# Maxima of one unit and a lead as own + relu(other - own), and V of twelve heads and a weight merge among the score tiles

## The reference

```python
q = _split(lora_linear(x, Wq, bq, Bq, Aq))
k = _split(lora_linear(x, Wk, bk, Bk, Ak))
v = _split(lora_linear(x, Wv, bv, Bv, Av))
scores = jnp.einsum('bhqd,bhkd->bhqk', q, k) * SCALE
attn = jax.nn.softmax(scores, axis=-1)
out = jnp.einsum('bhqk,bhkd->bhqd', attn, v)
...
return lora_linear(out, Wo, bo, Bo, Ao)
```

## Time and profile before

| what | value |
|---|---|
| median of three runs | 350.2 us (345.63 to 353.56) |
| the profiled execution | 349.53 us |
| its span, first to last instruction | 347.7 us |
| TensorE busy | 322.9 us of the span, 1919 matmuls |
| VectorE busy | 280.4 us, of which 150.3 us are the 128 maximum reductions |
| ScalarE busy | 241.9 us, of which 134.2 us are the 256 exponentials |
| GpSimd busy | 128.5 us |

### The profile page before, as it was taken

How to read it: one execution, slowest core, us unless ns; L and a number is a source line. 1 busy time by engine, 2 the same in 40 slices (tenths; PEclk the granted TensorE clock), 3 DMA queues, 4 the chain that set the end, 5 groups by cost and what they waited for, 6 DMA issues and landing times.

```text
span 347.7 us, 5546 instructions
## 1 busy us (share of the span) xinstructions
PE 322.9 (93%) x1919; PEld 141.8 (41%) x1919; DVE 280.4 (81%) x471; ACT 241.9 (70%) x465; POOL 128.5 (37%) x133
## 2 busy tenths in 40 slices
PE   7999789999999999999999899999998789699796
PEld 3753343222222222222222244359545645447695
DVE  6466998999999999999999345338689987988774
ACT  1576112888888898989888867994779323668694
POOL 5032018999300000000023001301699949994030
PEclk9999998999999999999999999999999969879899
DMA  7936855354132000000000000000000000000011
GB/s 216 326 51 129 144 166 86 63 117 84 21 78 45 3 0 3 0 3 0 0 3 1 3 1 2 0 2 0 1 2 0 1 0 2 0 2 0 1 62 60
DMA packets 14879, 14.57 MB, mean 42 GB/s; under 512 B 5060, under 2 KB 13191, under 8 KB 14663
## 3 DMA queue, kind: packets, MB, share of 16 engines
q1 hardware_dynamic: 12422, 12.09, 15.4%
q10 hardware_dynamic: 2176, 1.64, 1.6%
q0 software_dynamic: 256, 0.52, 0.9%
HBM read 5.78 MB, written 1.05 MB: 20 GB/s over the span
## 4 chain that ended last, share of the span: by engine, by line
PE 69%; DVE 14%; ACT 8%; POOL 5%; issue 3%; ACTq 0%; DVEq 0%; POOLq 0%
PE ps L1450 17%; PE ps L1436 13%; DVE mx L1126 9%; PE ps L1412 7%; PE ps L1582 6%; PE ps L1594 6%; PE ps L1363 4%; POOL pbuf L777 3%; PE ps L1567 3%; PE ps L1393 2%; PE ps L1626 2%; ACT ps L958 1%; PE ps L1352 1%; PE ps L1331 1%; ACT parts L898 1%
## 5 line engine op out<-in xcount | busy, mean ns | idle before, releaser
L1126 DVE TENSOR_REDUCE mx<-ps 128x1 f32<-128x1024 f32 x128 | 150.3, 1219 | 5.1 <-PE ps L1412 4.0
L913 ACT ACTIVATE pbuf<-ps 128x512 f32<-128x512 f32 x256 | 134.2, 604 | 24.6 <-PE ps L1436 23.6
L1436 PE MATMUL ps<-pack 64*128 64x512 f16 x256 | 75.9, 382 | 3.0 <-ACT pbuf L913 1.9
L1450 PE MATMUL ps<-pbuf,v_slot 128*32 128x512 f32 x512 | 68.0, 604 | 1.3 <-ACT parts L898 1.3
L1412 PE MATMUL ps<-pack 64*128 64x512 f16 x256 | 62.2, 388 | 4.5 <-DVE mx L1126 4.3
L1436 PEld LDWEIGHTS ps<-pack 64*128 64x128 f16 x256 | 18.8, 93 | 76.8 <-ACT pbuf L913 53.4
L777 POOL TENSOR_TENSOR pbuf<-wT 128x1024 f32<-128x1024 f32 (+3 forms) x32 | 48.2, 1533 | 4.7 <-ACT wT L987 4.7
L732 POOL COPY v_slot<-v_sb 128x512 f32<-128x512 f32 x8 | 4.8, 612 | 108.9 <-PE ps L1450 87.4
L708 POOL TENSOR_TENSOR rstd<-rstd,minus_half 128x2 f32<-128x2 f32 x16 | 11.4, 713 | 71.3 <-DVE rstd L1043 71.3
L1220 DVE SCALAR_TENSOR_TENSOR pack<-ps,g_unit,pack 128x512 f16<-128x512 f32 (+1 forms) x40 | 24.7, 640 | 14.5 <-ACT pack L970 14.5
L1582 PE MATMUL ps<-v_sb,w_nat 128*128 128x512 f16 (+1 forms) x160 | 32.7, 351 | 1.8 <-DVE v_sb L1212 1.8
(11 more groups left out here) (143 smaller groups left out, 370.4 us busy)
## 6 DMA issues: line engine op xcount, KB each, us to landing
w_nat<-in_L_ffn_w_dram SPq DMA_DIRECT2D x2, 1024.0 KB, 7.4
pack<-pbuf SPq DMA_DIRECT2D x24, 64.0 KB, 3.1
pack<-pack SPq DMA_DIRECT2D x3, 512.0 KB, 4.3
x_res<-in_L_attn_a_x_dram SPq DMA_DIRECT2D x4, 256.0 KB, 3.8
pack<-parts SPq DMA_DIRECT2D x16, 64.0 KB, 2.4
pack<-parts SPq DMA_DIRECT2D x32, 32.0 KB, 2.0
out_dram<-x_res SPq DMA_DIRECT2D x4, 256.0 KB, 2.1
w_nat<-in_L_attn_b_Wqkv_dram ACTq DMA_DIRECT2D x1, 768.0 KB, 6.3
```

Of the source, the lines that this page charges most:

```text
L913: act.activation(pbuf[:, c % 2, j, :], ps[:, b, :], ACT.Exp, scale=scale_reg).then_inc(drained[b], 1)
L1126: dve.tensor_reduce(mx[:, par, k:k + 1], ps[:, b:b + 2, :].rearrange("p b k -> p (b k)"), AX_X, ALU.max) \
L1436: pe.matmul(ps[:, b, :], k_group[rows, at, j, P * c:P * c + P].rearrange("p g t -> p (g t)"), q_rows[rows, at, qh, j, :].rearrange("p g t ...
L1450: ins = pe.matmul(ps[32 * j:32 * j + 32, PV_BANK, :], v_slot[:, qh, c, j, :], pbuf[:, c % 2, j, :], start=(c == 0), stop=(c == TT - 1))
```

## The change

For 23 maximum tiles (`is_signed`: all 16 of unit 0 and the seven of the lead), GpSimd first negates the queries in the half of the rows that only maxima read (`turn`). One matmul over all 128 rows then gives own minus other, a second over the 64 own rows gives own. ScalarE writes relu(other - own) to SBUF (`take_over_own`, two slots in `over_own`, which share the place of `tern1`), and VectorE adds that to the own scores and keeps the running maximum (`tensor_tensor_reduce`). The other 105 tiles stay.

V is cut in two: heads 0 to 3 (64 columns) beside unit 0's maxima and the lead, heads 4 to 15 (192 columns) as entries of the ring in front of certain score tiles of units 0 and 1 (`BESIDE_SCORES`), and so is Wo's merge. The ring's banks are now numbered by key over all units (`ring_keys`). The merge of Wv moves behind the projections 4 and 5. The shift of unit 0 lands by ScalarE's own DMA queue; on SP's queue the later shifts move ahead of some heads of groups 2 and 3. The load of Wqkv moves from ScalarE's queue to SP's. The clock-holding matmuls of the lead are five in one place, not two behind each of five tiles. ScalarE's loop over units is written out. `first_halves` lies in `parts` and not in `pbuf`, so that ScalarE's first exponentials no longer wait for the DMAs that read it. The waits for a group's rows stand where its first maximum tile is issued.

```diff
-    yield ("wt", V_)
     yield ("proj", 4)
     yield ("proj", 5)
+    yield ("wt", V_)
-    return [("proj", 6), ("proj", 7), *(("v", t) for t in range(TT)), ("wsum",), ("shift",), ("wt", O_)]
+    return [key for behind in (*BESIDE_FIRST_UNIT, *BESIDE_LEAD) for key in behind]
...
+BESIDE_FIRST_UNIT = [[] for _ in range(FILLS)]
+BESIDE_FIRST_UNIT[1] = [("proj", 6)]
+BESIDE_FIRST_UNIT[3] = [("proj", 7)]
+for _t, _k in enumerate(range(5, FILLS, 2)):
+    BESIDE_FIRST_UNIT[_k] = [("v", 0, _t)]
+BESIDE_LEAD = [[], [("shift", 0), ("wsum",)], [("v", 0, TT - 2)], [("v", 0, TT - 1)]]
+
+
+BESIDE_SCORES = {
+    **{(0, 4 * n + 4): ("v", 1, n) for n in range(TT - 2)},
+    (1, 4): ("v", 1, TT - 2), (1, 8): ("v", 1, TT - 1), (1, 12): ("wt", O_),
+}
...
+def ring_keys(u):
+
+    for s in range(STEPS):
+        if (u, s) in BESIDE_SCORES:
+            yield BESIDE_SCORES[u, s]
+        if s == SHIFT_AT and u < NU - 1:
+            yield ("shift", u + 1)
+        yield ("score", u, s)
...
+def is_signed(u, k):
+
+    return isinstance(u, int) and (u == 0 or u == 1 and k < LEAD)
...
+        def land_shift(eng, g, qh, u):
+
+            is_drained(eng, ("shift", u))
+            n = G * TT // 2
+            for r in (0, 1):
+                rows = SHIFT_ROWS[g // 2]
+                rows = slice(ROWS * r + rows.start, ROWS * r + rows.stop, rows.step)
+                eng.dma_start(q_rows[rows, g, qh, 2 * r:2 * r + 2, :].rearrange("o h t -> o (h t)"),
+                              m_rows[n * r:n * r + n, :]).then_inc(shift_landed, 16)
...
-            pack_heads(2, 0, 1)
-            land_shift(0, 0, 0)
-            pack_heads(2, 1, G - 1)
+            pack_heads(2, 0, 3)
+            land_shift(sp, 0, 1, 1)
+            pack_heads(2, 3, 1)
             repeat_group(2)
-            land_shift(0, 1, 1)
+            pack_heads(3, 0, 2)
+            land_shift(sp, 1, 0, 2)
+            pack_heads(3, 2, 2)
+            repeat_group(3)
...
+            is_drained(sp, ("wt", V_))
+            sp.dma_start(wqkv[:, :, :], a["L0_attn_b_Wqkv"].rearrange("(c p) h n -> p c (h n)", p=P)) \
+                .then_inc(wqkv_in, 16)
...
+            def turn(rows, g, qh, first, last):
+
+                at = q_rows[rows, g, qh, :, :].rearrange("p j t -> p (j t)")[:, first:last]
+                pool.tensor_scalar(at, at, -1.0, 0.0, ALU.mult, ALU.add).then_inc(turned, 1)
+                turns[0] += 1
+                pool.wait_ge(turned, turns[0])
+
+            for j in range(G):
+                pool.wait_ge(head_packed_by_pool[j], 32)
+                other = 1 - score_rows(j)
+                turn(slice(ROWS * other, ROWS * other + ROWS), 0, 0, HALF * j, HALF * j + HALF)
...
+            pool.wait_ge(second_half_repeated, 16)
+            turn(slice(ROWS, 2 * ROWS), 0, 1, 0, P * LEAD)
...
+            def take_over_own(u, k):
+
+                b = PAIR_BANKS[k % 2]
+                act.wait_ge(filled[b], base[b] + u * (FILLS // 2) + (k // 2 + 1))
+                act.activation(over_own[:, k % 2, :], ps[:, b + 1, :], ACT.Relu, scale=-1.0).then_inc(over_own_ready, 1)
...
+            for k in range(FILLS):
+                take_over_own(0, k)
+                if k == 3:
+                    evacuate_weight(V_)
+                for key in BESIDE_FIRST_UNIT[k]:
+                    beside(key)
+            act.wait_ge(scale_ready, 1)
+            scale_reg = act.alloc_register("exp_scale_bits")
+            act.reg_load(scale_reg, exp_scale[0:1, 0:1].bitcast(U32))
+            for k in range(LEAD):
+                take_over_own(1, k)
+                for key in BESIDE_LEAD[k] if k < len(BESIDE_LEAD) else ():
+                    beside(key)
+                if k == 1:
+                    land_shift(act, 0, 0, 0)
+                if k >= LEAD - 4 and k < LEAD - 1:
+                    exp_tile(0, k - (LEAD - 4))
+            exp_tile(0, G - 1)
+            for u in range(NU - 1):
                 for s in range(G, STEPS):
+                    if (u, s) in BESIDE_SCORES:
+                        beside(BESIDE_SCORES[u, s])
                     if s == SHIFT_AT:
                         copy_shift(u + 1)
                     exp_tile(u, s)
                 for s in range(G):
                     exp_tile(u + 1, s)
...
+                if is_signed(u, k):
+
+                    dve.wait_ge(over_own_ready, FILLS * u + k + 1)
+                    slot = over_own[:, k % 2, :]
+                    dve.tensor_tensor_reduce(slot, ps[:, b, :], slot, scale=1.0, scalar=LOWEST, op0=ALU.add, op1=ALU.max,
+                                             accum_out=mx[:, par, k:k + 1]).then_inc(drained[b], 1)
+                    return
                 dve.wait_ge(filled[b], base[b] + u * (FILLS // 2) + (k // 2 + 1))
                 dve.tensor_reduce(mx[:, par, k:k + 1], ps[:, b:b + 2, :].rearrange("p b k -> p (b k)"), AX_X, ALU.max) \
                     .then_inc(drained[b], 1)
...
+                _, part, t = key
+                first, n = V_PARTS[part]
+                cols = slice(HD * first, HD * first + HD * n)
...
-                out = to_fill(pe, key)[:, 0:D]
-                add_bias(out, "bv")
+                out = to_fill(pe, key)[:, 0:HD * n]
+                at = BIAS_AT["bv"]
+                pe.matmul(out, onesb[0:NPART, 0:P], bias_rows[:, at + cols.start:at + cols.stop], start=True, stop=False)
                 for d in range(DC):
-                    ins = pe.matmul(out, xT[:, d, P * t:P * t + P], wT[:, V_, d, :], start=False, stop=(d == DC - 1))
+                    ins = pe.matmul(out, xT[:, d, P * t:P * t + P], wT[:, V_, d, cols], start=False, stop=(d == DC - 1))
...
+                if is_signed(u, k):
+
+                    own = slice(ROWS * score_rows(j), ROWS * score_rows(j) + ROWS)
+                    pe.matmul(ps[:, b + 1, :], q_rows[:, g, qh, j, at], k_group[:, g, j, keys], start=True, stop=True)
+                    pe.matmul(ps[:, b, :], q_rows[own, g, qh, j, at], k_group[own, g, j, keys], start=True, stop=True) \
+                        .then_inc(filled[b], 1)
+                    return
...
             pe.wait_ge(second_half_repeated, 16)
+            pe.wait_ge(turned, G + 1)
             for k in range(LEAD):
```

More of the change, by code:

```diff
@@ L64 @@
 SHIFT_UNIT = 2.0 ** 15
+LOWEST = -3e38
+V_PARTS = ((0, G), (G, H - G))
 HALF_EXPONENT = 0x3F800000
@@ L252, in numbered @@
     return of
[L255 to L262, removed]
 class Banks:
@@ L284, in plan_banks @@
         banks.count[b] += NU * FILLS // 2
-    for i, b in enumerate(SCORE_BANKS):
-        banks.count[b] += (NU - 1) * RING_USES + ring_fills(STEPS - 1, i)
+    ring = itertools.cycle(SCORE_BANKS)
+    for u in range(NU):
+        for key in ring_keys(u):
+            banks.claim(key, next(ring))
     banks.count[PV_BANK] += NU
@@ L747, in _ @@
                     pool.wait_ge(tern_ready, 4 * n + c + 1)
+            for t in range(TT):
+                is_drained(pool, ("v", 1, t))
             for g in range(NG - 1):
@@ L1142, in _ @@
             cut_max(0, 0)
+            for k in range(LEAD):
+                take_max(1, k, 1)
             src = is_filled(dve, ("wsum",))
@@ L1147, in _ @@
                 .then_inc(drain_sem(("wsum",)), 1)
-            for k in range(LEAD):
-                take_max(1, k, 1)
             def unit_max(u, next_par):
@@ L1365, in project @@
                 ins.then_inc(fill_sem(key), 1)
-            def add_bias(out, which):
-                at, n = BIAS_AT[which], 512 if which == "qk" else D
-                pe.matmul(out, onesb[0:NPART, 0:P], bias_rows[:, at:at + n], start=True, stop=False)
             def project_v(key):
-                t = key[1]
-                if t == 0:
+                _, part, t = key
+                first, n = V_PARTS[part]
+                cols = slice(HD * first, HD * first + HD * n)
+                if part == 0 and t == 0:
                     is_drained(pe, ("wt", V_))
@@ L1440, in times_v @@
             def times_v(qh, u, c):
[L1442 to L1445 removed]
+                is_drained(pe, ("score", u, G * c + G - 1))
                 if c == 0:
@@ L1452, in times_v, with beside @@
                 ins.then_inc(pv_chunk if c < TT - 1 else filled[PV_BANK], 1)
-            side = [key for key in beside_max_pass() if key[0] in ("proj", "v")]
+            def beside(key):
+                if key[0] == "shift":
+                    pe.wait_ge(consts, 6)
+                    shift_rows(key[1])
+                else:
+                    setup[key[0]](key)
             for k in range(FILLS):
@@ L1503, in unit @@
                         elif fill >= FILLS and after is not None:
+                            if fill == FILLS and after[1] == 0:
+                                pe.wait_ge(group_packed[after[0]], group_count(after[0]))
+                                pe.wait_ge(group_repeated[after[0]], 48)
                             max_tile(*after, fill - FILLS)
```

177 lines of the change are left out of this document (56 added, 121 removed).

## The result

| | before | changed kernel |
|---|---|---|
| median of the runs | 351.31 us (4 runs, 345.63 to 353.56) | 358.62 us (4 runs, 357.54 to 360.38) |
| ratio | | 1.031 (95% interval 1.017 to 1.045) |
| the profiled execution, its span | 349.53, 347.7 us | 357.54, 355.7 us |
| unit 0's maxima are cut | 52.47 | 50.19 |
| first product with V | 63.16 | 65.18 |

A forecast was written before the change was run, and what follows sets the result against it. VectorE was taken to bound the units, with TensorE close behind. Front -3.0, lead -1.5 and V with Wo's merge in the units +9.1 gave +4.6 us on the profiled 349.53, so 354 us; range 347.5 to 360.

The forecast's parts named there:

- unit 0's maxima, to the cut: 16 signed tiles and what breaks their round: 18.8 us against 21.57, so the cut comes 3 us earlier (2 to 4).
- lead, with the first V product: Unit 1's seven tiles, held by ScalarE's queue: 1.5 us won (0.5 to 2.5); one V entry before the first product.
- units 0 and 1 from there: V of heads 4-15 adds 0.87 us to each of eight chunks, Wo's merge 2.1 us: +9.1 us (5.9 to 10.5).
- tail: After the units: Wqkv's load, needed there, priced at nothing.
- TensorE's clock falls: Rival, chance 0.13: 1.2 GHz in the lead costs 1.7 us, in the pass 0.43 us a round, 3.4 in eight: 359 us.
- the 59.5 of the forecast: End of the lead: the first product with V expected near 59.5 us.
- The signed round: Maximum pass: two tiles through TensorE, ScalarE and VectorE take 2.14 us, 1.07 a tile against 1.16, no engine full.
- Half rate: Rival, chance 0.05: VectorE's fused sum takes 1.16 us for 512 elements, pass 22.4 us, front wins 0.5: 358 us.
- GpSimd's negations: Before the maximum tiles: five instructions of 1.2 to 1.6 us, priced at nothing; about 1.2 us if the first took twice as long.
- Part 3: V of heads 4-15 and Wo's merge as score-ring entries cost units 0 and 1 9.1 us; 64-column V costs the pass nothing.

The follow-up runs named there:

- hold22: Changed kernel plus two clock-holding matmuls ahead of the first maximum tile and of each of V's eight products in pass and lead; 357.14 us, ratio 1.025.
- Hold12: Changed kernel plus matmuls: two ahead of the first maximum tile, one ahead of each V product of the pass, two in the lead; 359.53 us, ratio 1.035.
- Sp_shift: Changed kernel with the first shift's two DMA issues back on SP's queue; 359.31 us, ratio 1.034.
- no_keep: Changed kernel without the five clock-holding matmuls ahead of the first score; 360.29 us, ratio 1.037.
- hold: Changed kernel plus two matmuls ahead of each of the eight V products of the maximum pass and the lead; 357.73 us, ratio 1.036.
- hold1: Changed kernel plus one matmul ahead of each of the six V products of the maximum pass, none in the lead; 357.15 us, ratio 1.027.
- plain: Changed kernel with plain reductions everywhere (no relu, no negation), V of heads 4 to 15 still in the units; 358.57 us, ratio 1.035.
- plain_v_pass: Changed kernel with plain reductions and V of all 16 heads in the maximum pass and lead; 348.45 us, ratio 1.007.
- v_pass: Changed kernel with V of all 16 heads in the maximum pass and lead, none in the units, signed tiles kept; 351.45 us, ratio 1.015.

## Why the prediction was wrong

| term | forecast | measured |
|---|---|---|
| unit 0's maxima, to the cut | -3.0 | -2.28 |
| lead, with the first V product | -1.5 + 0.87 | +4.30 |
| units 0 and 1 from there | +9.1 - 0.87 | +8.47 |
| tail | 0 | -2.5 |

**The step that failed is the clock.** The sum for the front was made at 2.4 GHz, and the rival "TensorE's clock falls" had 0.13, with "in the pass TensorE has 2 x 0.65 + 0.55 = 1.85 us of profile-busy time in each 2.14" against it. The profile of the changed kernel shows that busy time (1.68 to 1.94 of 2 us), and the clock fell. The rival is what came: 359 us, measured 358.6. That the two figures agree is partly luck, since the tail's clock gave 2.5 us back, and the rival's parts were sized differently: a round grew by 1.12 us, not 0.43, since at 1.2 GHz TensorE is the bound of it, but only the last rounds were hit, some 2.0 us (40.35 to the cut took 9.84, at full clock 3 x 2.13 + 1.45 = 7.84 with the 1.45 of hold22). The lead paid more than the 1.7: 14.99 us against 12.58 - 1.08 = 11.5 of hold22 less its matmuls, 3.5 us. Together 5.5 us; the first product was 5.7 later than the 59.5 of the forecast.

**The signed round** was priced at 2.14 us and is 2.13 between VectorE's tiles at 2.4 GHz; sum, relu and read-out were right to 0.02 us each. "Half rate" falls: 0.691 us against 0.686 for the plain sum. The Trainium skill's page "Vector Engine (DVE) Microarchitecture Reference", section "Points that are easy to get wrong", states the halving for two non-bf16 sources in SBUF; one was in PSUM here, and the trace agrees in that 0.691 us shows no halving.

**The gain of the pass was sized right and put down to the wrong thing.** I set 16 signed tiles against the old 21.57 us: 18.8 us, a gain of 2.8 that the sum took as 3.0. Hold12, at full clock up to its cut, took 18.89 us for them (VectorE's timeline, first sum and cut):

```profile
30.51 0.69 DVE L1169 CUSTOM_DVE_ANT_0 tern<-ps,tern 128x512 f32<-128x512 f32 x1 [1.22 <-ACT tern L925]
...
49.40 0.17 DVE L1180 TENSOR_SCALAR m_parts<-mx 128x16 f16<-128x16 f32 x1
```

But with plain tiles in the new order the cut came as early (49.95 and 50.30): the pass began 1.3 to 1.6 us earlier in both, which I had not counted, and a plain tile takes 1.14 us where nothing breaks the row. At full clock a signed tile's 1.07 is worth 0.07 us a tile, about 1 us in 16; hold12's cut, 0.55 to 0.9 us ahead of the plain ones, bears that out.

**The lead**: I had it held by ScalarE's queue and left the clock-holding matmuls out "on both sides". Sp_shift shows that the queue isn't on the path, no_keep that the five matmuls are: 2.1 us at 1.2 GHz. At 2.4 they take 1.18, and V's last two products 0.62 each, all in TensorE's own list, which the sum had left out. So the lead was mis-sized at full clock too: 11.5 us, by hold22 less its matmuls, against the 10.1 of the forecast. What came behind the first exponential was right: in hold22 the fourth started 3.27 us later, 3.30 was forecast.

**GpSimd's negations** at nothing: so in the changed kernel, but in two of the eight profiles with signed tiles (hold and hold1) TensorE waited 0.4 us for the first one, and a fall of the clock followed that cost another 1.6; that the wait brought it on is not shown.

**Part 3 was right.** V chunks took 3.36 us (3.26 forecast), seven of them behind the first product 7 x 0.97 = 6.8, and the chunk with Wo's merge 4.74, +2.35 (2.1). The plain kernels give 9.0 for moving V; of that 2.4 is plain's lead at half clock (13.90 us against 10.56, less the 0.97 of the V entry in it), and plain_v_pass loses 1.1 to a spell of its own behind its first product. That V with 64 columns costs the pass "nothing" was true of TensorE's time and false of its clock.

## What to carry over

Work that fills TensorE's waits may be what keeps its clock up: before moving it away, look which stretch then runs at 1.2 GHz, and who bounds that stretch at 1.2. A tile that is VectorE's (1.14 us whatever the clock) is safer there than one that needs TensorE, ScalarE and VectorE in a row. And set a new tile's time against the old tile in the new order, not against the old stretch with all that broke it.

## What the runs showed of the hardware

The clock fell with TensorE nearly always busy in the profile (1.94 of 2 us in the stretch before), not in a gap: the longest wait of the round was 0.32 us. In the leads of v_pass, hold1 and hold12 it fell 0 to 2 us behind waits of 1.38, 0.88 and 1.03 us for VectorE; hold22 waited 0.94 us at that place and kept 2.4 GHz. The Trainium skill's page "TensorE: Matmul & The Clock Gate", section "HAM oscillation — how this bites in real kernels", shows the fall behind long waits for DMA; no such wait stands ahead of the changed kernel's fall. And neighbouring matmuls of 512 columns that change between 128 and 64 rows start 0.32 us apart at 2.4 GHz, where two on 64 rows each start together and the next 0.23 us later. The Trainium skill's page "TensorEngine Tiling (Array Packing)", section "Key Properties", says that a change of the tiling mode drains TensorE; the trace fits that, with some 0.1 us a change as an estimate from 0.32 and 0.23, though no run sets the change apart from other causes.
